# Graph network on one Trainium2 core: SyncE fetches four pairs of tiles per layer row by row, by row numbers in registers

## The chip, the core and the metric

The kernel runs on one core of one Trainium2 chip. The metric is the device time of one execution in microseconds (us). Five engines run their own instruction streams and meet at semaphores: TensorE (PE in the profile), VectorE (DVE), ScalarE (ACT), GpSimd (POOL) and SyncE (SP), which in this kernel only issues DMAs.

## The reference

Three layers of a relational graph network over 6250 nodes of 256 numbers and 100000 edges, sorted by target node, then a layer norm.

```python
ew = edge_attr @ edge_w + edge_b
inv_cnt = [1.0 / max(segment_sum(edge_type == i, dst), 1.0) for i in range(3)]
for l in range(3):
    residual = x
    msg = relu(x[src] * ew)
    out = zeros((n, 256))
    for i in range(3):
        h = segment_sum(msg * (edge_type == i)[:, None], dst) * inv_cnt[i][:, None]
        out = out + h @ weights[l, i]
    out = out + x @ roots[l] + biases[l]
    x = residual + relu(out)
return layernorm(x0 + x)
```

## The kernel before

The edges are cut into 782 tiles of 128, handled as 391 pairs per layer. One step of a layer handles one pair (`q` in the code; `l` is the layer).

- **GpSimd gathers.** For each tile one indirect DMA (`gather`, L620 to L626) fetches the 128 rows `x[src]`, 1 KB each, by the row numbers in a column of `idx`, into one of twelve places of the ring `xg` (`XR = 12`, so six pairs). Before it refills a place it waits on `s_sc` until TensorE has summed the pair that lay there. GpSimd does nothing else once the kernel has started up.
- **TensorE** computes the edge weights of a pair (L771), with the transposed edge attributes from `at`; **VectorE** waits for both gathers and multiplies the rows in place by these weights (L1092, called the product below); **ScalarE** applies relu (L694); TensorE sums the rows per target node and relation with a 0/1 matrix `S` (L790, `collect`); VectorE adds these sums to the accumulator `acc` (L948), whose column it takes from a number that it has loaded into a register (L1082).
- **Blocks.** 49 blocks of 128 target nodes own 384 columns each in both halves of `acc`. When the last tile that touches a block is in (`starts[k]`), TensorE multiplies the block's sums by the weights (L842), VectorE finishes the nodes, SyncE stores them to `x` of the next layer, and ScalarE clears the block's columns (L721). The block that finishes first (`k = 0` in the order of finishing, at step 14) is the short one at the end of `acc`, columns from `384 * (NB - 1)`.
- **SyncE** runs in step with TensorE, since most of its DMAs wait for a semaphore of TensorE. Per two steps it issues, in layer 0, one load of edge attributes (L523) and one store of their transposed form (L529), and in layers 1 and 2 one load of that form (L535). Per block it issues one load of the block's x (L541) and one store of the result (L555), in layer 2 also a second load (L547). Its DMAs are issued in program order: one that waits, or takes long to issue, holds up all behind it.
- **Between layers** GpSimd waits until all stores of the new x have landed, and only then gathers again.

The order of the tiles is written by `plan()`. Steps are in the same place in every engine's program, and nothing but semaphores sets the pace.

Of the kernel before, what the change touches and what calls it, by code (L numbers as in the profile page):

```python
# [62 lines left out]
def gnn_program(nc, x_in, src, dst, edge_attr, edge_type, weights, roots, biases, edge_w, edge_b,  # L63
# [5 lines left out]
    DVE = mybir.EngineType.DVE  # L69
# [15 lines left out]
    PAD = 1000000  # L85
    BR = 196
# [25 lines left out]
    with ctx:  # L112
# [104 lines left out]
        s_st, s_sq, s_no = sem("s_st"), sem("s_sq"), sem("s_no")  # L217
        s_dm, s_d2, s_hz = sem("s_dm"), sem("s_d2"), sem("s_hz")
# [15 lines left out]
        def tile(n):  # L234

            return head_tile(order[n // 4]) + n % 4

# [263 lines left out]
        def _(eng):  # L501
# [55 lines left out]
            for g in range(3):  # L557
                load_attr(g)

            def fast():  # L560
                for l in range(L):
                    late = (13, 9, 15)[l]
                    for q in range(-4, end):
                        if l == 0 and q % 2 == 0:
                            if 3 <= q // 2 + 4 < NG:
                                load_attr(q // 2 + 4)
                            if 0 <= q // 2 < NG:
                                keep_attr(q // 2)
                        if l and q % 2 == 0 and q // 2 + 2 < NG:
                            reload_attr(l, q // 2 + 2)  # L570
                        if q == 0:
                            for i in range(TB if l else 0):
                                eng.wait_ge(s_xo[i], 16 * uses(l, i, TB, NB))
                            if l == 0:
                                load_weights(l)
                            for k in range(XB):
                                load_x(l, k)
                            if l == L - 1:
                                load_x0(0)
                                load_x0(1)  # L580
                        if q == 8 and l:
                            load_weights(l)
                        for k in starting(q, 8 if l else 12):
                            if k + XB < NB:
                                load_x(l, k + XB)
                        for k in starting(q, 9):
                            if l == L - 1 and k + 2 < NB:
                                load_x0(k + 2)
                        for k in starting(q, late):
                            store(l, k)  # L590
# [10 lines left out]
        def _(eng):  # L601
# [18 lines left out]
            def gather(l, j):  # L620
                n = l * NT + j
                if n >= XR:
                    eng.wait_ge(s_sc, 2 * ((n - XR) // 2 + 1))
                eng.indirect_dma_start(  # L624
                    out=xg[:, n % XR, :], out_offset=None, in_=xs[l],
                    in_offset=bass.IndirectOffsetOnAxis(ap=idx[:, tile(j):tile(j) + 1], axis=0)).then_inc(s_g[n % XR], 16)  # L626

            eng.wait_ge(s_src, 16)
            for j in range(XR):
                gather(0, j)  # L630

            def fast():
                for l in range(L):
# [3 lines left out]
                    for j in range(0 if l else XR, NT):  # L637
                        gather(l, j)
# [5 lines left out]
        def _(eng):  # L644
# [42 lines left out]
            def fast():  # L687
                for l in range(L):
                    for q in range(-6, end):
                        Q = l * NP + q  # L690
                        if 0 <= q < NP:
                            eng.wait_ge(s_m, Q + 1)
                            v = xg[:, (2 * Q) % XR:(2 * Q) % XR + 2, :]
# [23 lines left out]
                        if l < L - 1:  # L717
                            for k in starting(q, 5 if l else 7):
                                eng.wait_ge(s_d1, NB * l + k + 1)
                                a, b = columns(blocks[k])  # L720
# [12 lines left out]
        def _(eng):  # L733
# [41 lines left out]
            def collect(l, q):  # L775
# [11 lines left out]
                for i in range(2):  # L787
                    n = 2 * V + i
                    for h in range(2):
                        last = eng.matmul(pA[V % 2][:, 192 * i + 96 * h:192 * i + 96 * h + 96],  # L790
                                          xg[:, n % XR, 128 * h:128 * h + 128], S[:, slot(l, 2 * q + i), :],
# [81 lines left out]
        def _(eng):  # L873
# [200 lines left out]
            def fast():  # L1074
                for l in range(L):
                    todo = {}
                    for q in range(-6, end):
# [8 lines left out]
                        if 0 <= q < NP:  # L1086
                            for i in range(2):
                                n = 2 * Q + i
                                eng.wait_ge(s_g[n % XR], 16 * (n // XR + 1))
                            eng.wait_ge(s_e, Q + 1)  # L1090
                            v = xg[:, (2 * Q) % XR:(2 * Q) % XR + 2, :]
# [83 lines left out]
```

## Time and profile before

| | before |
|---|---|
| median of 3 runs (lowest to highest) | 2993.76 us (2991.76 to 2998.16) |
| the profiled execution's own time | 2995.98 us |
| its span, first to last instruction | 2994.3 us |
| granted TensorE clock, mean | 0.956 |
| busy share of the span: PE, PEld, DVE, ACT, POOL | 87%, 80%, 71%, 43%, 74% |
| gathers (DMA_INDIRECT on POOL) | 2346, of 0.95 us each |
| DMA issues on SP | 1147 |

The own time lies 1.68 us above the span, and 2.2 us above the median of the runs. Shares of busy time count only what the engines themselves compute: the time in which a sequencer loads a register, waits for a semaphore or issues a DMA is not in them, and SP has no busy time at all for that reason.

### The profile page before, as it was taken

To read this page: it belongs to the slowest core of one execution; us is meant where nothing else is said; L and a number is where in the kernel's file an instruction comes from. 1 tells how busy PE (TensorE), PEld (TensorE's weight loads), DVE (VectorE), ACT (ScalarE), POOL (GpSimd) and SP (SyncE) were. 2 spreads that over 40 slices of the span, in tenths; PEclk is the share of its full clock that TensorE was granted. 3 is DMA by queue.
4 is the path that set the end of the run, shared out by engine and by line. 5 is a ranking of instruction groups with operands and counts; after the bars stand their busy time and mean duration, and the time that the engine had idled before them with its cause. 6 is when DMAs were issued, how large, how long until landed. Compare 5 with 4: busy or idle time off the path is not lost. (4 is left out here: it accounts for less than half of the span.)

```text
span 2994.3 us, 59606 instructions
## 1 busy us (share of the span) xinstructions
PE 2611.1 (87%) x18388; PEld 2409.2 (80%) x18388; DVE 2127.0 (71%) x5989; ACT 1279.4 (43%) x2735; POOL 2227.1 (74%) x2363
## 2 busy tenths in 40 slices
PE   7899999999999788888898888878888888888887
PEld 6888888988889677778787788867778888877786
DVE  6777777777777566666666666656767777777776
ACT  6667777767666323233333333323223233233332
POOL 6777777777777677777777777767777777777775
PEclk9999999999999899999999999989999999999999
DMA  6555655555565445445554555444555555555553
GB/s 170 156 159 156 160 159 158 161 158 160 160 161 159 142 142 146 143 146 146 146 147 146 147 146 146 144 136 145 149 148 152 154 149 156 150 156 150 157 152 111
DMA packets 317059, 451.39 MB, mean 151 GB/s; under 512 B 156127, under 2 KB 203718, under 8 KB 316742
## 3 DMA queue, kind: packets, MB, share of 16 engines
q0 software_dynamic: 112608, 307.65, 36.5%
q1 hardware_dynamic: 203604, 139.69, 16.3%
q8 instruction: 156, 2.56, 0.3%
q14 instruction: 161, 1.32, 0.1%
q10 hardware_dynamic: 530, 0.18, 0.0%
HBM read 402.46 MB, written 44.82 MB: 149 GB/s over the span
## 5 line engine op out<-in xcount | busy, mean ns | idle before, releaser
L624 POOL DMA_INDIRECT xg<-x,idx x1564 | 1481.9, 948 | 503.5 <-issue 340.1
L694 ACT ACTIVATE xg<-xg 128x512 f32<-128x512 f32 x1173 | 739.3, 630 | 1668.3 <-DVE xg L1092 1654.4
L790 PE MATMUL bank<-S,xg 128*128 128x96 f32 x9384 | 1331.0, 287 | 131.0 <-DVE acc L948 97.3
L1092 DVE TENSOR_TENSOR xg<-xg,bank 128x512 f32<-128x512 f32 x1173 | 805.2, 686 | 791.6 <-issue 344.4
L790 PEld LDWEIGHTS bank<-S,xg 128*128 128x128 f32 x9384 | 1195.8, 199 | 201.7 <-ACT xg L694 173.1
L771 PE MATMUL bank<-wsb,at 128*128 128x256 f32 x4692 | 917.9, 319 | 175.4 <-DVE xg L1092 143.5
L624 POOL DMA_INDIRECT xg<-in_x_dram,idx x782 | 742.9, 950 | 243.7 <-issue 163.9
L771 PEld LDWEIGHTS bank<-wsb,at 128*128 128x128 f32 x4692 | 690.0, 198 | 255.6 <-issue 108.6
L948 DVE TENSOR_TENSOR acc<-acc,bank 128x192 f32 x2346 | 813.9, 347 | 30.2 <-DVE acc L948 13.8
L842 PE MATMUL bank<-W,acc 128*128 128x256 f32 (+1 forms) x1764 | 496.0, 405 | 3.0 <-DVE acc L948 3.0
L842 PEld LDWEIGHTS bank<-W,acc 128*128 128x128 f32 (+1 forms) x1764 | 380.4, 255 | 5.4 <-DVE acc L948 3.5
L929 DVE TENSOR_TENSOR S<-bank,kr 128x384 f32<-128x384 f32 x588 | 323.0, 549 | 0.0
L713 ACT ACTIVATE oh_a<-iota,lo 128x128 bf16<-128x128 bf16 x782 | 266.1, 388 | 0.0
L965 DVE SCALAR_TENSOR_TENSOR t<-bank,inv,t 128x256 f32<-128x256 f32 (+1 forms) x441 | 209.1, 474 | 15.8 <-PE bank L842 15.5
L842 PE MATMUL bank<-W,xT 128*128 128x256 f32 (+1 forms) x588 | 170.2, 416 | 0.0
L747 PE MATMUL bank<-ident,hs 128*64 128x128 f32 x782 | 121.7, 280 | 19.0 <-ACT xT L702 15.8
L842 PEld LDWEIGHTS bank<-W,xT 128*128 128x128 f32 (+1 forms) x588 | 111.9, 209 | 10.7
L668 ACT ACTIVATE at<-bank 64x512 fp32r<-64x512 f32 x196 | 112.3, 573 | 4.6 <-PE bank L747 4.5
L747 PEld LDWEIGHTS bank<-ident,hs 128*64 128x64 f32 x782 | 86.4, 120 | 24.8 <-DVE hs L885 18.8
L785 PE MATMUL bank<-oh_b,oh_a 128*128 128x12 bf16 x782 | 80.1, 174 | 12.3 <-issue 8.2
L721 ACT ACTIVATE acc<-zcol 128x768 f32<-128x768 f32 (+1 forms) x98 | 81.4, 831 | 14.2 <-PE bank L842 14.2
L815 PE MATMUL bank<-ident,xblk 128*128 128x128 f32 (+1 forms) x294 | 59.0, 284 | 23.3 <-ACT at L668 23.2
(64 smaller groups left out, 687.2 us busy)
## 6 DMA issues: line engine op xcount, KB each, us to landing
at<-attr_t SPq DMA_DIRECT2D x390, 128.0 KB
xg<-x,idx POOLq DMA_INDIRECT x1564
attr_t<-at SPq DMA_DIRECT2D x195, 128.0 KB
xg<-in_x_dram,idx POOLq DMA_INDIRECT x782
hs<-in_edge_attr_dram SPq DMA_DIRECT2D x194, 64.0 KB
x<-t SPq DMA_DIRECT2D x96, 128.0 KB
xblk<-x SPq DMA_DIRECT2D x96, 128.0 KB
xblk<-in_x_dram SPq DMA_DIRECT2D x48, 128.0 KB
```

Source lines behind the costliest of these rows:

```text
L624: eng.indirect_dma_start(out=xg[:, n % XR, :], out_offset=None, in_=xs[l], in_offset=bass.IndirectOffsetOnAxis(ap=idx[:, tile(j):tile(j) + ...
L668: eng.activation(at[0:64, g % TR, 0:w], pT[0:64, 0:w], ACT.Copy).then_inc(s_atc, 1)
L694: eng.activation(v, v, ACT.Relu).then_inc(s_r, 1)
L713: eng.activation(oh_a[:, j % AR, :], iota[:, 1:129], ACT.Sign, bias=lo[:, tile(j):tile(j) + 1]).then_inc(s_oh, 1)
L747: last = eng.transpose(pT[0:64, 128 * i:128 * i + 128], hs[:, g % 3, i, :], ident[:, :])
L771: last = eng.matmul(pE[Q % 2][:, 256 * i:256 * i + 256], at[:, sl, c:c + 128], wsb[:, p, :], start=(p == 0), stop=(p == 1))
L790: last = eng.matmul(pA[V % 2][:, 192 * i + 96 * h:192 * i + 96 * h + 96], xg[:, n % XR, 128 * h:128 * h + 128], S[:, slot(l, 2 * q + i), : ...
L842: last = eng.matmul(o, a, W[:, 2 * (r % 4) + h, :], start=(h == 0), stop=(h == 1))
L929: eng.tensor_tensor(S[:, at4:at4 + w, :], steps_of[:, 1:WK + 1].unsqueeze(1).to_broadcast([128, w, WK]), kr[:, c:c + w].unsqueeze(2).to_br ...
L948: eng.tensor_tensor(a, a, pA[V % 2][:, 192 * i:192 * i + 192] .rearrange("p (h w) -> p h w", h=2), ALU.add).then_inc(s_acc, 1)
L965: return eng.scalar_tensor_tensor(tt, products(k, m), inv[0:n, 3 * blocks[k] + r:3 * blocks[k] + r + 1], tt, ALU.mult, ALU.add)
L1092: eng.tensor_tensor(v, v, pE[Q % 2][:, :].rearrange("p (i d) -> p i d", i=2), ALU.mult).then_inc(s_m, 1)
```

## The change

Per layer, four of the 391 pairs (113, 204, 295 and 386, `BY_ROW`) are no longer gathered by GpSimd. SyncE fetches their 256 rows by one DMA of one row (1 KB) each. It first loads the pair's row numbers from DRAM into SBUF (`load_list`, two DMAs of 512 bytes), then reads four of these numbers into registers at a time, computes a byte offset from each, and issues a DMA with that offset (`load_rows`). The 64 groups of four rows of a pair are spread over 84 of SyncE's steps: for pair 113 over steps 26 to 109, for a later one from 4 steps behind the pair before it to 4 steps ahead of its own.

The rows go into columns of `acc` that belong to the short block, which is finished at step 14: 256 columns in both halves hold the pair, the 128 behind them the row numbers. So ScalarE clears this block at the layer's last step and no longer right behind its products. GpSimd leaves the four pairs out and numbers its ring places by the pairs that are left; VectorE waits for such a pair on `s_row`, and product, relu and sums work on `acc` in place of `xg`.

```diff
+    BY_ROW = (113, 204, 295, 386)
...
+        def pool_pair(l, q):
+            return l * (NP - len(BY_ROW)) + q - sum(p < q for p in BY_ROW)
+        pairs = [(l, q) for l in range(L) for q in range(NP) if q not in BY_ROW]
+        row_buf = acc[:, :, 384 * (NB - 1):384 * (NB - 1) + D]
+        def rows_of(l, q):
+            if q in BY_ROW:
+                return row_buf
+            a = 2 * pool_pair(l, q) % XR
+            return xg[:, a:a + 2, :]
+        def row_list(i, h):
+            a = 384 * (NB - 1) + D
+            return acc[32 * h:32 * h + 1, i % 2, a:a + 128].bitcast(I32)
...
+            def load_list(l, i):
+                for h in range(2):
+                    a = 128 * tile(2 * BY_ROW[i] + h)
+                    eng.dma_start(row_list(i, h), src[a:a + 128].rearrange("(q p) -> q p", q=1)).then_inc(s_sr[i % 2], 16)
+            def load_rows(l, i, c):
+                if c == 0:
+                    eng.wait_ge(s_sr[i % 2], 32 * (l * len(BY_ROW[i % 2::2]) + i // 2 + 1))
+                if c == 0 and i:
+                    eng.wait_ge(s_sc, l * NT + 2 * (BY_ROW[i - 1] + 1))
+                if c == 32 and i + 1 < len(BY_ROW):
+                    load_list(l, i + 1)
+                h, e = c // 32, 4 * (c % 32)
+                _, vals = nc.values_load_multi_w_load_instructions(
+                    row_list(i, h)[:, e:e + 4], engines=[SP], min_val=0, max_val=N - 1,
+                    skip_runtime_bounds_check_because="a node's number")
+                for r, v in enumerate(vals):
+                    eng.dma_start(row_buf[e + r:e + r + 1, h, :], xs[l][bass.ds(v, 1), :]).then_inc(s_row[l], 16)
+            def row_turn(q):
+                for i, p in enumerate(BY_ROW):
+                    b = BY_ROW[i - 1] + 4 if i else p - 87
+                    if b <= q < b + 84 and (q == b or (q - b) * 64 // 84 > (q - b - 1) * 64 // 84):
+                        return i, (q - b) * 64 // 84
+                return None
...
+                        if q == BY_ROW[0] - 89:
+                            eng.wait_ge(s_d1, NB * l + 1)
+                            load_list(l, 0)
+                        if row_turn(q):
+                            load_rows(l, *row_turn(q))
...
-            def gather(l, j):
-                n = l * NT + j
-                if n >= XR:
-                    eng.wait_ge(s_sc, 2 * ((n - XR) // 2 + 1))
+            def gather(l, q, i):
+                P = pool_pair(l, q)
+                n = 2 * P + i
+                if P >= XR // 2 and i == 0:
+                    before, pair = pairs[P - XR // 2]
+                    eng.wait_ge(s_sc, before * NT + 2 * (pair + 1))
...
-                            for k in starting(q, 5 if l else 7):
+                            for k in ([0] if q == NP - 1 else []) + [k for k in starting(q, 5 if l else 7) if k]:
                                 eng.wait_ge(s_d1, NB * l + k + 1)
+                                if k == 0:
+                                    eng.wait_ge(s_sc, l * NT + 2 * (BY_ROW[-1] + 1))
...
-                            for i in range(2):
-                                n = 2 * Q + i
+                            if q in BY_ROW:
+                                eng.wait_ge(s_row[l], 16 * 256 * (BY_ROW.index(q) + 1))
+                            for i in range(0 if q in BY_ROW else 2):
+                                n = 2 * pool_pair(l, q) + i
                                 eng.wait_ge(s_g[n % XR], 16 * (n // XR + 1))
```

SyncE in layer 0, steps 24 to 28, before (`hs` holds raw edge attributes, `attr_t` their transposed form in DRAM, `xblk` a block's x, `t` a block's result):

```order
L529 DMA attr_t<-at 64x512 [waits s_atc]
L523 DMA hs<-in_edge_attr_dram 128x4x32 [waits s_tr]
L529 DMA attr_t<-at 64x512 [waits s_atc]
L541 DMA xblk<-in_x_dram 128x256 [waits s_rd]
L555 DMA x<-t 106x256 [waits s_rd]
L523 DMA hs<-in_edge_attr_dram 128x4x32 [waits s_tr]
```

The same place in the changed program, behind the two DMAs for the row numbers (its lines L544, L550 and L562 are L523, L529 and L541 of before):

```order
L544 DMA hs<-in_edge_attr_dram 128x4x32 [waits s_tr]
L550 DMA attr_t<-at 64x512 [waits s_atc]
L593 TENSOR_LOAD acc [waits s_sr0]
L597 ISA
L597 DMA acc<-in_x_dram 1x256
L597 ISA
L597 DMA acc<-in_x_dram 1x256
L597 ISA
L597 DMA acc<-in_x_dram 1x256
L597 ISA
L597 DMA acc<-in_x_dram 1x256
L562 DMA xblk<-in_x_dram 128x256 [waits s_rd]
```

Between the attribute DMAs of two steps there now stand one or two such groups of nine instructions: one register load, then four times a calculation (ISA) and a DMA of one row. The block's load and store stand behind a group too.

GpSimd, start and gathers of all layers, before:

```order
L624 DMA xg<-in_x_dram,idx 128x256 x12
L493 TENSOR_LOAD flag
L493 ISA x2
L494 COMPARE_AND_BRANCH
L624 DMA xg<-in_x_dram,idx 128x256 x770
L624 DMA xg<-x,idx 128x256 x1564
```

and changed:

```order
L679 DMA xg<-in_x_dram,idx 128x256 x12
L514 TENSOR_LOAD flag
L514 ISA x2
L515 COMPARE_AND_BRANCH
L679 DMA xg<-in_x_dram,idx 128x256 x762
L679 DMA xg<-x,idx 128x256 x1548
```

Eight gathers per layer are gone; nothing takes their place on GpSimd.

VectorE at pair 386 of layer 0, before:

```order
L1082 TENSOR_LOAD brow
L1092 TENSOR_TENSOR xg<-xg,bank 128x512 [waits s_e,s_g5,s_g4]
L948 ISA [waits s_acc,s_sc]
L948 TENSOR_TENSOR acc<-acc,bank 128x2x96
L929 TENSOR_TENSOR S<-bank,kr 128x384 [waits s_sc]
```

and changed:

```order
L1141 TENSOR_LOAD brow
L1153 TENSOR_TENSOR acc<-acc,bank 128x2x256 [waits s_e,s_row0]
L1007 ISA [waits s_acc,s_sc]
L1007 TENSOR_TENSOR acc<-acc,bank 128x2x96
L988 TENSOR_TENSOR S<-bank,kr 128x384 [waits s_sc]
```

The product of such a pair stands where it stood and has its size; it waits for SyncE's rows in place of two gathers.

## Rows read from the trace of the kernel before

**Rows 1.** Timeline of POOL: start us, us, what [idle before <- releaser].

```profile
1003.17 0.95 POOL L624 DMA_INDIRECT xg<-x,idx  x1 [12.90 <-DMA x<-t]
...
1500.67 0.95 POOL L624 DMA_INDIRECT xg<-x,idx  x1 [0.30 <-PE bank L790]
1501.92 0.95 POOL L624 DMA_INDIRECT xg<-x,idx  x1 [0.30 <-issue]
1503.17 0.95 POOL L624 DMA_INDIRECT xg<-x,idx  x1 [0.30 <-issue]
...
1979.39 0.94 POOL L624 DMA_INDIRECT xg<-x,idx  x1 [0.30 <-issue]
```

**Rows 2.** Waits of POOL, 1010 to 1980 us: us in total, times, longest us.

```profile
POOL xg L624 <- issue: 169.1, 555, 0.3
POOL xg L624 <- PE bank L790: 67.6, 222, 0.3
```

**Rows 3.** Busy time by stretch: layer 0, layer 1.

```profile
20.00:990.00 970.00, 898.29 (x7161) 846.78 (x7160) 745.62 (x2465) 675.48 (x1692) 730.50 (x771) 0.98 0.59 159
1003.00:1980.00 977.00, 842.54 (x5543) 765.51 (x5544) 655.11 (x1599) 294.20 (x486) 738.91 (x782) 0.95 0.50 146
```

**Rows 4.** Waits of DVE, 1010 to 1980 us.

```profile
DVE xg L1092 <- DMA xg<-x,idx: 127.2, 150, 9.3
```

**Rows 5.** Timeline of PE, sums of one pair each, 1499 to 1506 us.

```profile
1499.29 1.03 PE L790 MATMUL bank<-S,xg 128*128 128x96 f32 x8
...
1501.58 1.03 PE L790 MATMUL bank<-S,xg 128*128 128x96 f32 x8
```

**Rows 6.** Timeline of all engines: products at the end of layer 0.

```profile
984.41 0.69 DVE L1092 TENSOR_TENSOR xg<-xg,bank 128x512 f32<-128x512 f32 x1 [3.18 <-DMA xg<-in_x_dram,idx]
...
986.20 0.68 DVE L1092 TENSOR_TENSOR xg<-xg,bank 128x512 f32<-128x512 f32 x1
...
988.07 0.69 DVE L1092 TENSOR_TENSOR xg<-xg,bank 128x512 f32<-128x512 f32 x1 [0.37 <-issue]
...
990.66 0.69 DVE L1092 TENSOR_TENSOR xg<-xg,bank 128x512 f32<-128x512 f32 x1
```

**Rows 7.** DMA issues on SP by line: duration ns min/median/max, first and last start us.

```profile
L523 SPq DMA_DIRECT2D hs<-in_edge_attr_dram x196: 368/377/1035, 2.7 to 971.5; - x196
L529 SPq DMA_DIRECT2D attr_t<-at x196: 445/516/1703, 20.2 to 990.1; - x196
L535 SPq DMA_DIRECT2D at<-attr_t x392: 444/450/1367, 1001.7 to 2961.6; - x196
L541 SPq DMA_DIRECT2D xblk<-x x98: 310/334/435, 1003.7 to 2911.2; - x98
L541 SPq DMA_DIRECT2D xblk<-in_x_dram x49: 336/584/1352, 24.1 to 939.2; - x49
L555 SPq DMA_DIRECT2D x<-t x98: 298/438/1611, 80.9 to 1992.6; - x98
```

**Rows 8.** A one-row DMA on ACT's queue; register loads and calculations of sequencers.

```profile
L651 ACTq DMA_DIRECT2D acc<-in_L_gnn_edge_b_dram x1: 597/597/597, 3.2 to 3.2; - x1
...
L493 SPq TENSOR_LOAD <-flag x1: 468/468/468, 14.5 to 14.5; - x1
...
L493 SPq FUSED_REGOPS  x1: 188/188/188, 15.0 to 15.0; - x1
...
L1082 DVEq TENSOR_LOAD <-brow x588: 339/560/1225, 18.4 to 2976.3; - x196
...
L948 DVEq FUSED_REGOPS  x2346: 46/46/46, 24.1 to 2981.5; - x196
```

**Rows 9.** Timeline of SP in layer 0, two DMAs behind each other.

```profile
771.00 0.38 SPq L523 DMA_DIRECT2D hs<-in_edge_attr_dram  x1
771.42 0.52 SPq L529 DMA_DIRECT2D attr_t<-at  x1
```

**Rows 10.** Waits of SP, whole span.

```profile
SPq L535 <- PE bank L771: 1070.8, 274, 9.1
SPq L523 <- PE bank L747: 698.6, 191, 8.7
```

More of the change, by code:

```diff
@@ L68, in gnn_program @@
     AX = mybir.AxisListType
-    DVE = mybir.EngineType.DVE
+    DVE, SP = mybir.EngineType.DVE, mybir.EngineType.SP
     N, E, D, R, L = 6250, 100000, 256, 3, 3
@@ L217, in gnn_program @@
         s_st, s_sq, s_no = sem("s_st"), sem("s_sq"), sem("s_no")
+        s_sr = sems("s_sr", 2)
+        s_row = sems("s_row", L)
         s_dm, s_d2, s_hz = sem("s_dm"), sem("s_d2"), sem("s_hz")
@@ L618, in _ @@
                                   base=b, pattern=[[-1, 128]], channel_multiplier=1).then_inc(s_df, 1)
-            def gather(l, j):
-                n = l * NT + j
-                if n >= XR:
-                    eng.wait_ge(s_sc, 2 * ((n - XR) // 2 + 1))
+            def gather(l, q, i):
[4 more added lines that the diff above has]
+                    eng.wait_ge(s_sc, before * NT + 2 * (pair + 1))
+                c = tile(2 * q + i)
                 eng.indirect_dma_start(
                     out=xg[:, n % XR, :], out_offset=None, in_=xs[l],
-                    in_offset=bass.IndirectOffsetOnAxis(ap=idx[:, tile(j):tile(j) + 1], axis=0)).then_inc(s_g[n % XR], 16)
+                    in_offset=bass.IndirectOffsetOnAxis(ap=idx[:, c:c + 1], axis=0)).then_inc(s_g[n % XR], 16)
             eng.wait_ge(s_src, 16)
-            for j in range(XR):
-                gather(0, j)
+            for l, q in pairs[0:XR // 2]:
+                gather(l, q, 0)
+                gather(l, q, 1)
             def fast():
@@ L636, in fast @@
                             eng.wait_ge(s_xo[i], 16 * uses(l, i, TB, NB))
-                    for j in range(0 if l else XR, NT):
-                        gather(l, j)
+                    for q in range(0 if l else XR // 2, NP):
+                        if q not in BY_ROW:
+                            gather(l, q, 0)
+                            gather(l, q, 1)
             both(eng, "gpsimd", fast)
@@ L692, in fast @@
                             eng.wait_ge(s_m, Q + 1)
-                            v = xg[:, (2 * Q) % XR:(2 * Q) % XR + 2, :]
+                            v = rows_of(l, q)
                             eng.activation(v, v, ACT.Relu).then_inc(s_r, 1)
@@ L787, in collect @@
                 for i in range(2):
-                    n = 2 * V + i
                     for h in range(2):
                         last = eng.matmul(pA[V % 2][:, 192 * i + 96 * h:192 * i + 96 * h + 96],
-                                          xg[:, n % XR, 128 * h:128 * h + 128], S[:, slot(l, 2 * q + i), :],
+                                          rows_of(l, q)[:, i, 128 * h:128 * h + 128], S[:, slot(l, 2 * q + i), :],
                                           start=True, stop=True)
@@ L1086, in fast @@
                         if 0 <= q < NP:
[L1087 to L1088 removed]
+                            if q in BY_ROW:
+                                eng.wait_ge(s_row[l], 16 * 256 * (BY_ROW.index(q) + 1))
+                            for i in range(0 if q in BY_ROW else 2):
+                                n = 2 * pool_pair(l, q) + i
                                 eng.wait_ge(s_g[n % XR], 16 * (n // XR + 1))
                             eng.wait_ge(s_e, Q + 1)
[L1091 removed]
+                            v = rows_of(l, q)
                             eng.tensor_tensor(v, v, pE[Q % 2][:, :].rearrange("p (i d) -> p i d", i=2),
```

## The prediction

> **What bounds the kernel now.** The busy shares point at PE (87%), and for this change they mislead. I read the timeline of GpSimd first, then its waits, then the same for the engines that use the rows.
>
> GpSimd's gathers start 1.25 us apart, 0.95 us in the gather and 0.30 us until the next one [rows 1]. Over layer 1, the first starts at 1003.17 us and the last of 782 at 1979.39 us: 976.22 / 781 = 1.250 us each, so not one came late. The waits say the same: none of the 777 idle stretches of that layer was longer than 0.3 us, whether it is put down to PE or to nothing [rows 2]. The busy share of 74% is only 0.95 / 1.25 with the layer ends taken off. The three layers hold 2346 such periods, 2932 us of the 2994.3.
>
> No other engine is at its limit. In layer 1 PE computes 843 of 977 us, VectorE 655, in layer 0 PE 898 of 970 [rows 3]. VectorE waited 127 us in layer 1 for rows still under way [rows 4]. And the places of the ring are free early. Counted from the layer's first gather, the one at 1500.67 us is tile (1500.67 - 1003.17) / 1.25 = 398, the first of pair 199, and may go once pair 193 is summed. The sums on PE at 1499.29 us are pair 195's, those at 1501.58 us pair 196's [rows 5]. So pair 194 was done too; by the pace of 2.3 to 2.5 us per pair, pair 193 had been done for 4 to 6 us.
>
> **What the change removes.** Eight gathers per layer, 24 in all, from the queue that sets the pace: 24 x 1.25 = **30.0 us**. A step of TensorE and VectorE must then take 2.5 x 387 / 391 = 2.47 us on average in place of 2.50.
>
> **Can the others take one pair more between two gathers?** At a row-by-row pair they have an extra pair's work while rows keep coming at 2.5 us per pair. How fast they go with rows at hand shows behind a late gather: after an idle time of 3.18 us the products start 1.79, 1.87 and 2.59 us apart, 2.08 us on average [rows 6]. So with one pair extra, the product of the pair behind it starts 2 x 2.08 - 2.50 = 1.7 us late, and each later pair makes up 0.4 us. That is less than the 4 us by which the ring's places are free early, so GpSimd isn't stopped: no cost there. Only at a layer's end is it seen, because pair 386 is followed by just four pairs: 1.7 - 3 x 0.42 = 0.4 us late at pair 390, **1.2 us** for three layers.
>
> **What the change adds to SyncE** is the term on which all rests, and the trace has no DMA by a register's value.
>
> - Register load of four numbers: VectorE's takes 0.56 us, SyncE's only one (of one number) 0.47 us; the gap behind an instruction is 0.04 us (771.00 + 0.38 to 771.42). I take 0.51 with its gap [rows 8, 9].
> - Calculation: 0.046 us on VectorE; with its gap 0.08. SyncE's own, longer one took 0.19 right behind a load, so at most 0.15 more per group [rows 8].
> - One-row DMA: SyncE's loads of a block's x, the same 1 KB rows into SBUF, take 0.334 us for 128 rows when nothing was issued just ahead, 0.31 at the least (the block of 106 rows) [rows 7]. The only DMA of one row is ScalarE's, 0.597 us, one of six issued back to back beside SyncE's own at the start [rows 8]. These are the bounds, 0.31 and 0.60. I take 0.33, the row with the same kind of transfer, with the queue in the state in which a register load just ahead leaves it; with its gap 0.37.
>
> One row is then 0.08 + 0.37 = 0.45 us, a group 0.51 + 4 x 0.45 = 2.31 us, a pair 64 x 2.31 = 148 us.
>
> SyncE's own work in 84 steps, medians plus gaps: in layer 0 42 x (0.377 + 0.516 + 0.08) + 10.5 blocks x (0.584 + 0.438 + 0.08) = 41 + 12 = 53 us; in layer 1 42 x 0.49 + 10.5 x 0.85 = 29 us; in layer 2, with a second load of 0.37 per block, 33 us [rows 7]. The 84 steps last 84 x 2.47 = 208 us. Layer 0: 148 + 53 = 201. Layers 1 and 2: 177 and 181. It fits, by 7 us in layer 0 and some 29 in the others, and before this work SyncE mostly waited: 1070.8 and 698.6 us on its two main waits [rows 10]. So all of the new work lies in time in which SyncE waited.
>
> The cover is thin, so its limits matter. Behind a group stand the attribute loads for TensorE and, in layer 0, for ScalarE. A group is 2.3 us, so such a load goes out up to 2.3 us later (4.6 where two groups stand together); layer 1 has it for step q + 3 at step q, some 7 us ahead. With a one-row DMA of x us, layer 0 falls behind within the 84 steps from (208 - 53) / 64 = 2.42 us per group, which is x = 0.36, and over the whole 91 steps (225 us, own work 57) from 2.62 us, x = 0.41. Layer 1 bears x = 0.51, layer 2 0.49.
>
> The rest costs nothing. The product on `acc` has the size of that on `xg` (0.69 us [rows 6]). ScalarE's clear of the short block moves to the last step, behind the last relu, where ScalarE waits for the last block anyway; the next layer asks for it only with all other clears. The load of a list is two short DMAs per pair, in front of work that is 32 groups away. The 3072 rows, 3 MB, were moved before too.
>
> **Sum.** 2994.3 - 30.0 + 1.2 = 2965.5 us of span, 2967.2 of own time (1.68 above). The profiled run was 2.2 us above the median, so the median to expect is **2965.0**.
>
> The Trainium skill ("DMA: Bandwidth & Descriptors", the table on the faster descriptor path, in the section "Why a DMA increments its semaphore by 16 and not by 1") speaks against my price: it gives 512 sequencer cycles for a DMA copy on the generations before that path. With the 1.2 GHz of "Advanced Engine Details and Errata", section "Clock Domains", that is an estimate of 0.43 us. This trace half agrees: the attribute loads take 0.45 us, the loads of x 0.33. By it a group would be 2.7 us and the kernel some 20 us above my sum.
>
> **Rivals.**
>
> 1. *SyncE is late in layer 0 alone* (x between 0.41 and 0.46). For it: the attribute loads at 0.450 us, the stores at 0.438 and 0.516 behind another DMA [rows 7]. Over a cycle of 91 steps SyncE's excess sets the pace. At x = 0.43 a group is 0.51 + 4 x 0.55 = 2.71 us, the cycle 57 + 173 = 230 against 225: 4 x 5 = 20 us, time 2985. At x = 0.435 the 30 us are used up (2994); at 0.46 it is 3009. Against it: there the DMA waits behind a large one; here nothing large stands ahead. Chance 0.15, of which two thirds below 2988. The skill's 0.43 us, above, would be this case.
> 2. *SyncE becomes the bound everywhere* (the other side). One mechanism: a one-row DMA costs SyncE 0.60 us, as ScalarE's did [rows 8]. A group is 0.51 + 4 x 0.72 = 3.39 us, a pair 217. Cycles of 57 + 217 = 274, 32 + 217 = 249 and 36 + 217 = 253 us stand against 225: 4 x (49 + 24 + 28) = 404 us, time 3370. It is slower than before from x = 0.435 on, by layer 0 alone, and from x = 0.51 on the other layers are over their limit too. Attribute loads would be late, and TensorE wait for them. For it: the only row of its form. Against it: its neighbours on that queue took 0.45 with 32 rows, so 0.15 of it may be the queue's state; and a register's value may add time that no row shows. Chance 0.16.
> 3. *The extra pair does stop GpSimd*, or rows come late by a few us and the product waits: each of the 12 pairs gives back 1 to 2.5 us. Time 2977 to 2994. Against it: the ring's 4 us and more. Chance 0.06.
> 4. *No effect*: GpSimd's period stretches, since it gathers less but the DMA engines or its own issue slow down. Nothing for it; the period was 1.25 in all layers. Chance 0.03.
>
> The forecast itself, 2961 to 2974, has 0.60.
>
> **How the numbers follow.** A measurement of this kernel tells about 0.2% (6 us) from no change. Faster: 0.60, two thirds of rival 1, most of rival 3: 0.75. Same: the rest of rival 3, rival 4 and a piece of rival 1: 0.07. Slower: 0.18. The range has to take in most of rival 1 and rival 3: 2961 to 3005 holds 0.81.
>
> **What would show it.** Right: 2322 gathers, still 1.25 us apart in every layer; gathering of each layer 10 us shorter; a group of nine instructions on SyncE near 2.3 us, its one-row DMA near 0.33 us; SyncE still waiting for PE on its attribute DMAs within the 84 steps; VectorE with no wait to speak of at the four products; layer ends within a us of before. Wrong: gaps on POOL above 0.3 us that end with PE, and PE waiting for attribute loads, above all in layer 0, where the margin is 7 us in 208; or a wait of VectorE for the rows.

## The result

| | before | changed |
|---|---|---|
| median (lowest to highest) | 2992.78 us (2991.76 to 2998.16), 4 runs | 3093.73 us (3087.56 to 3098.62), 4 runs |
| the profiled execution's own time | 2995.98 us | 3096.11 us |
| its span | 2994.3 us | 3094.3 us |
| granted TensorE clock, mean | 0.956 | 0.936 |
| gathers on POOL | 2346 | 2322 |

The changed kernel is slower: ratio 1.0332, 95% interval 1.0309 to 1.0356. The forecast was 2965.0 us, the range ended at 3005. The experiments ran on four chips. On those of e6 to e9 and of e10 to e12 the kernel before takes 2994.2 and 2994.8 us, so their times can be set beside each other. On those of e1 to e4 and of e5 the same kernel takes 3602 and 3605 us; of these runs only ratios, differences between themselves and the lengths of single instructions are used.

**Where the 100 us lie.** The starts of the gathers again give the layers, from the first to the last. Layer 0 takes 1081.1 us instead of 984.8 (+96.3), the pause behind it 23.6 instead of 13.9 (+9.8), layer 1 967.3 instead of 976.2 (-8.9), the next pause 14.5 instead of 15.7 (-1.2), layer 2 983.0 instead of 979.7 (+3.3), the tail 20.2 instead of 19.5 (+0.7). The sum is +100.0, the difference of the two spans. So layer 1 shows the gain that was forecast for every layer, and layer 0 a loss ten times as large.

Waits of the changed kernel in layer 0, 5 to 1086 us (us in total, times, longest us):

```profile
ACT hs L718 <- DMA hs<-in_edge_attr_dram: 264.7, 124, 6.1
DVE hs L944 <- ACT hs L718: 185.7, 103, 5.3
POOL xg L679 <- PE bank L849: 159.1, 158, 5.8
```

Before, GpSimd had no wait of more than 0.3 us in layer 1 [rows 2] and few in layer 0. Here it waits up to 5.8 us for a place in its ring, that is for the sums on PE. The first row shows what is late ahead of PE: ScalarE waits 124 times for edge attributes that SyncE loads from DRAM.

The waits of SP over the whole span, to be read beside [rows 10] (L544 is L523 of before, L556 is L535):

```profile
SPq L556 <- PE bank L831: 159.5, 83, 9.6
SPq L544 <- PE bank L807: 67.8, 26, 8.3
```

SyncE's idle time on its two main waits, 1769 us before, is 227 us now. Within the second window of row loads, 316 to 581 us, what is left of it is this:

```profile
SPq L550 <- ACT at L726: 2.4, 5, 0.8
SPq L544 <- PE bank L807: 0.5, 2, 0.3
```

With 2.9 us of waiting in 265 us SyncE is the bound there. In the chain that ended last SP's queue (SPq) has as large a share as PE; in that of the kernel before it does not occur:

```profile
SPq 28%; PE 28%; DMA 14%; issue 13%; POOL 12%; DVE 3%; ACT 2%; DVEq 0%
```

**One stall, followed.** Timelines of SP, ACT, PE and POOL in layer 0 of the changed kernel (start us, us, what; loads of registers have no row of their own in this view and show as gaps):

```profile
426.64 0.37 SPq L562 DMA_DIRECT2D xblk<-in_x_dram  x1
428.28 1.50 SPq L597 DMA_DIRECT2D acc<-in_x_dram  x4
429.83 0.38 SPq L576 DMA_DIRECT2D x<-t  x1
430.26 0.43 SPq L544 DMA_DIRECT2D hs<-in_edge_attr_dram  x1
430.73 0.68 SPq L550 DMA_DIRECT2D attr_t<-at  x1
433.27 1.54 SPq L597 DMA_DIRECT2D acc<-in_x_dram  x4
434.86 0.41 SPq L544 DMA_DIRECT2D hs<-in_edge_attr_dram  x1
```

```profile
433.35 0.31 ACT L718 ACTIVATE hs<-hs 128x128 fp32r<-128x128 f32 x1 [4.91 <-DMA hs<-in_edge_attr_dram]
```

```profile
435.15 0.20 PE L845 MATMUL bank<-oh_b,oh_a 128*128 128x12 bf16 x2 [3.84 <-ACT oh_a L771]
```

```profile
432.92 0.94 POOL L679 DMA_INDIRECT xg<-in_x_dram,idx  x1 [0.30 <-issue]
437.48 0.94 POOL L679 DMA_INDIRECT xg<-in_x_dram,idx  x1 [3.62 <-PE bank L849]
```

The view shows no wait of SP here: each gap is a register load and the first address behind it, 1.27 us from 427.01 to 428.28 and 1.86 us from 431.41 to 433.27, and four rows take 1.50 us and more. The attribute load behind them goes out at 430.26. ScalarE, idle for 4.91 us, gets its attributes at 433.35. Its next work stands behind them in program order, and PE, idle for 3.84 us, waits for that work until 435.15. Only then come the sums that free a place of the ring, and GpSimd stands for 3.62 us from 433.86 on. An attribute load serves two pairs, 5.0 us of GpSimd's time; in this window SyncE has 42 of them in 265 us, one every 6.3 us.

**The price of the load.** Durations of SP's register loads by stretch (min/median/max in ns): layer 0, window of the first pair and of the second; layer 1, the same two.

```profile
L593 SPq TENSOR_LOAD <-acc x64: 465/827/1241, 80.4 to 300.9; - x64
...
L593 SPq TENSOR_LOAD <-acc x64: 1062/1666/1815, 315.9 to 577.3; - x64
...
L593 SPq TENSOR_LOAD <-acc x64: 485/738/753, 1176.0 to 1381.6; - x64
...
L593 SPq TENSOR_LOAD <-acc x64: 1032/1307/1328, 1401.7 to 1620.9; - x64
```

The loads of SyncE have 0.47 us, without the gap, in the prediction. None of the four medians is near it, and the second pair's loads are about 0.6 us longer than the first pair's in layer 1 and 0.8 in layer 0. The rest of a row is cheap, in the first pair's window (L597, three instructions for each of 256 rows):

```profile
L597 SPq FUSED_REGOPS  x256: 37/37/48, 81.3 to 302.7; - x128
L597 SPq MOVE acc<-in_x_dram x256: 29/29/38, 81.4 to 302.8; - x128
L597 SPq DMA_DIRECT2D acc<-in_x_dram x256: 224/228/297, 81.5 to 302.9; - x128
```

From the first load to the last row, a group of four takes 2.54 us (mean of 64) in the windows of pairs 1 and 3 of layer 0 and 3.20 in those of pairs 2 and 4; the means of the loads in them are 0.82 and 1.49 us. In layer 1 the groups take 2.36 and 2.93 us. These windows show when GpSimd stood. What its gathers start later than 1.25 us behind the one before, called its gaps below, adds up to 2, 45, 12 and 41 us in the four windows of layer 0, at most 0.5 us in each of those of layer 1, and 1, 8, 2 and 5 us in layer 2.

### The profile page after: what moved, and what is told of

Its sections match the earlier page's. It is cut to its first block, busy times and chain, and to the rows that moved or that the text cites. A ratio compares the mean times of both kernels' runs of the same rounds, so it can differ in the third digit from the quotient of the medians.

```text
span 3094.3 us, 69601 instructions
## 1 busy us (share of the span) xinstructions
PE 2634.8 (85%) x18388; PEld 2450.5 (79%) x18388; DVE 2140.4 (69%) x5989; ACT 1280.9 (41%) x2735; POOL 2205.3 (71%) x2339
## 4 chain that ended last, share of the span: by engine, by line
SPq 28%; PE 28%; DMA 14%; issue 13%; POOL 12%; DVE 3%; ACT 2%; DVEq 0%
PE bank L849 14%; POOL xg L679 12%; SPq L597 11%; SPq L593 11%; DMA xg<-x,idx 9%; PE bank L901 6%; PE bank L831 6%; DMA hs<-in_edge_attr_dram 2%; SPq L550 2%; DMA at<-attr_t 2%; SPq L544 1%; DVE acc L1007 1%; SPq L556 1%; PE bank L807 1%; DVE xg L1153 1%
## 5 line engine op out<-in xcount | busy, mean ns | idle before, releaser
L752 ACT ACTIVATE xg<-xg 128x512 f32<-128x512 f32 x1161 | 729.1, 628 | 1464.9 <-DVE xg L1153 1460.6
L849 PEld LDWEIGHTS bank<-S,xg 128*128 128x128 f32 x9288 | 1209.9, 203 | 154.0 <-ACT xg L752 132.1
L1153 DVE TENSOR_TENSOR xg<-xg,bank 128x512 f32<-128x512 f32 x1161 | 795.2, 685 | 582.4 <-DMA xg<-x,idx 301.3
L831 PE MATMUL bank<-wsb,at 128*128 128x256 f32 x4692 | 936.3, 324 | 210.1 <-DVE xg L1153 104.0
L831 PEld LDWEIGHTS bank<-wsb,at 128*128 128x128 f32 x4692 | 705.9, 202 | 284.4 <-DMA at<-attr_t 113.4
L901 PE MATMUL bank<-W,acc 128*128 128x256 f32 (+1 forms) x1764 | 503.8, 410 | 3.1 <-DVE acc L1007 3.1
L944 DVE TENSOR_TENSOR hs<-hs 128x128 f32<-128x128 f32 x196 | 57.0, 291 | 190.8 <-ACT hs L718 189.8
L718 ACT ACTIVATE hs<-hs 128x128 fp32r<-128x128 f32 x196 | 59.8, 306 | 270.4 <-DMA hs<-in_edge_attr_dram 269.3
L845 PEld LDWEIGHTS bank<-oh_b,oh_a 128*128 128x128 bf16 x782 | 51.7, 106 | 90.4 <-ACT xg L752 74.0
```

The source lines that it names most:

```text
L752: eng.activation(v, v, ACT.Relu).then_inc(s_r, 1)
L831: last = eng.matmul(pE[Q % 2][:, 256 * i:256 * i + 256], at[:, sl, c:c + 128], wsb[:, p, :], start=(p == 0), stop=(p == 1))
L901: last = eng.matmul(o, a, W[:, 2 * (r % 4) + h, :], start=(h == 0), stop=(h == 1))
L1153: eng.tensor_tensor(v, v, pE[Q % 2][:, :].rearrange("p (i d) -> p i d", i=2), ALU.mult).then_inc(s_m, 1)
```

## The experiments

Pairs 113, 204, 295 and 386 are called pairs 1 to 4. Pairs 1 and 3 have their row numbers in the first half of `acc`, pairs 2 and 4 in the second.

**e1, e2: without the loads.** e1 leaves out the register loads, the row DMAs and the wait for them; e2 issues the row DMAs with row numbers fixed when the program is built, without loads or calculations.

```diff
-                for r, v in enumerate(vals):
+                for r, v in enumerate(range(97 * c, 97 * c + 4)):       # e2
-                    eng.dma_start(row_buf[e + r:e + r + 1, h, :], xs[l][bass.ds(v, 1), :]).then_inc(s_row[l], 16)
+                    pass                                                # e1
```

> Leaves out the row loads of the four pairs and their register loads: SyncE does none of the new work, VectorE does not wait for rows, GpSimd gathers as in the change. Theory A (GpSimd's gain is real and SyncE's lateness alone eats it): 2322 gathers 1.25 us apart in all layers, time 2963 to 2967. Rival (the shorter gather list gains nothing, because another engine or the extra pair stops GpSimd): 2980 or more, with gaps on POOL that end with PE.

> Fetches rows with fixed numbers, so it leaves out the register loads and calculations; the same 3072 one-row DMAs are issued. Theory A (the register load, 0.9 to 1.15 us on average against 0.51 in the prediction's sum, is what makes SyncE late): without it a group is some 1.1 to 1.3 us, layer 0 has 208 - 53 - 80 = 75 us to spare, time as without rows, 2963 to 2970. Rival (the 3072 small DMAs themselves, through contention with attribute loads and gathers, cost the time): above 3000.

Measured: e1 3576.55 us, ratio 0.9927 (0.9911 to 0.9944); e2 3620.69 us, ratio 1.0058 (1.0041 to 1.0075). Leaving out 24 gathers is worth 26 us on this chip, so most of the 30 us is a real gain. The gathers were not 1.25 us apart throughout, as expected; GpSimd waited 515 us for the sums on PE and 262 us for what the profile calls remote. With the 3072 row DMAs the time is 44 us longer than in e1. That is the side of the rival: on this chip these DMAs cost time without any register load. e9 and e11 below show no such cost on the chips on which the kernel before takes 2994 us.

**e3, e5: where the list starts.** The second half of `acc` lies 18846 columns of 4 bytes, 75384 bytes, behind the first, which is 8 past a multiple of 16. The first list starts at byte 74752 of `acc` in its partition, a multiple of 16; so the second starts 8 bytes past one. (That `acc` itself starts at a multiple of 16 isn't on record; e12, with all four starts, bears it out.) e3 moves the second list by two columns, so that both start at a multiple; e5 moves the first one instead, so that neither does.

```diff
-            a = 384 * (NB - 1) + D
+            a = 384 * (NB - 1) + D + 2 * (i % 2)          # e3
+            a = 384 * (NB - 1) + D + 2 * ((i + 1) % 2)    # e5
```

> One edit: the second list of row numbers lies two columns further on, so that it starts at a multiple of 16 bytes as the first does. In the profile of the change loads from the first list take 0.49 to 0.74 us and from the second 1.06 to 1.31 us (layer 1). Theory A (a load of four numbers that crosses a 16-byte boundary is read twice): loads of the second and fourth pair fall by 0.57 us, layer 0 loses its 45 to 50 us of gaps at each of these two pairs down to the 6 to 12 us of the others, time 2995 to 3025. Rival (loads of the second list are slow for another reason, as the steps they fall in or the semaphore before them): loads stay above 1 us and the time at 3090.

> One edit: the first list is moved two columns on too, so that both lists start 8 bytes behind a multiple of 16 (all else as in the change). Theory A (a load of four numbers that crosses a 16-byte boundary is read twice, 0.57 us more): in layer 1 loads of the first and third pair rise from 0.49 to 0.74 to 1.06 to 1.31 us, like those of the second and fourth; layer 0 loses some 45 us at each of its pairs, and on a chip like the one of the change's profile the time goes from 3094 to 3150 to 3180 us. Rival (the second list's loads are slow for another reason): loads of the first and third pair stay, time as the change, 3094.

Measured: e3 3749.78 us, ratio 1.0398 (1.0381 to 1.0415); e5 3944.43 us, ratio 1.0945 (1.09 to 1.0989). All 768 loads of each, e3 first:

```profile
L595 SPq TENSOR_LOAD <-acc x768: 3/707/1510, 97.7 to 3723.8; - x192
```

```profile
L595 SPq TENSOR_LOAD <-acc x768: 3/1239/2694, 97.5 to 3919.9; - x192
```

The start of the list decides the length of the load, and the half of `acc` that it is in does not: with all lists off the median is 1.24 us, with none 0.71, and the times are 195 us apart. The loads of 3 ns and the like, 92 of e3's below 0.1 us, stand only in the profiles of these chips and stay unexplained. The changed kernel itself wasn't run on them, so what e3 gives back there is not known; its 4.0% above the kernel before misses the 2995 to 3025 us that were expected. e10 is the same kernel on a chip of the faster kind.

**e4: rows in layers 1 and 2 only,** with the lists as in the change. The pairs and windows stand in a table by layer, whose first row is empty here.

```diff
-    BY_ROW = (113, 204, 295, 386)
+    ROWS = [[], [(113, 26, 84), (204, 117, 84), (295, 208, 84), (386, 299, 84)], [(113, 26, 84), (204, 117, 84), (295, 208, 84), (386, 299, 84)]]
```

> Layer 0 gathers all its pairs as before; rows go by SyncE in layers 1 and 2 alone, the second list unaligned as in the change. Theory A (layer 0 is where the time goes; layers 1 and 2 gain): layer 0 as before, layer 1 some 10 us shorter, layer 2 some 2 us longer as in the profile of the change to 7 shorter, time 2975 to 2990. Rival (the loss has a part that is in all layers and only shows in layer 0): above 3000.

Measured: 3712.28 us, ratio 1.0319 (1.0284 to 1.0354). Layer 0 took 1199.1 us, 9 more than in e1, with its eight gathers more, and layers 1 and 2 took 54 and 61 us more than in e1. With aligned lists (e3) they took 35 and 39 us more, with fixed rows (e2) 15 and 12. So on that chip rows cost in every layer, which is the rival's side, while in the main comparison layer 1 gained. For the main comparison this run decides nothing; e7 has its aligned form on the chip of e6.

**e6: the change again**, on the chip of e7 to e9.

> The changed kernel itself (its four row windows written as a table), as the reference point for the runs beside it. Both theories: a register load of 0.5 to 0.75 us from the first list and 0.57 us more from the second; the time 3 to 6 per cent above the kernel before. If it stands at the ratio 1.033 of the main comparison, the costs on this chip can be read in the same terms; if it is well above that, only differences between the runs of this call count.

Measured: 3094.44 us, ratio 1.0352 (1.0325 to 1.0378), the main result once more; layers of 1077.1, 967.9 and 981.9 us.

**e10: both lists aligned, nothing else** (the edit of e3).

> The changed kernel with the second list two columns further, so that both lists start at a multiple of 16 bytes; four numbers to a load, rows in all three layers. Theory (the loss is SyncE's in layer 0 and scales with the length of its loads): the loads of pairs 2 and 4 fall from 1.07 to 1.8 us to those of pairs 1 and 3, layer 0 loses only what pairs 1 and 3 lost in the changed kernel, twice over: 2 x (6 + 12) = some 35 us instead of 110, layer 2 its 15 us; the time 3094 - 75 - 12, about 3005 us, ratio 1.00 to 1.01. Rival (SyncE's time is short in layer 0 whatever the list, the loss moves to the other pairs): layer 0 still 60 us and more too long, ratio 1.015 to 1.03.

Measured: 3000.3 us, ratio 1.0016 (1.0006 to 1.0026). Loads of pairs 1 and 2 in layer 0:

```profile
L595 SPq TENSOR_LOAD <-acc x64: 465/760/1201, 80.5 to 301.1; - x64
...
L595 SPq TENSOR_LOAD <-acc x64: 487/748/1171, 316.2 to 537.6; - x64
```

The groups now take 2.53 to 2.54 us in layer 0, and its gaps fall from 111 us (e6) to 34; the kernel before has 8. Two columns are worth 94 us, almost the whole loss. (e6 and e10 ran on two chips, on which the kernel before differs by 0.6 us.) The rival, that the loss only moves to the other pairs, falls. GpSimd's and ScalarE's waits in layer 0 (5 to 980 us) are still there, smaller:

```profile
ACT hs L719 <- DMA hs<-in_edge_attr_dram: 185.2, 105, 4.5
POOL xg L680 <- PE bank L850: 68.0, 128, 5.3
```

**e8: the load ahead of its step's transfers,** lists as in the change. **e11: the same with both lists aligned.**

```diff
                     for q in range(-4, end):
+                        if row_turn(l, q):
+                            load_numbers(l, *row_turn(l, q))
                         if l == 0 and q % 2 == 0:
                             if 3 <= q // 2 + 4 < NG:
                                 load_attr(q // 2 + 4)
```

`load_numbers` holds the wait for the list and the register load, taken out of `load_rows`, which keeps the addresses and the DMAs.

> The changed kernel with each register load moved to the head of its step, ahead of the attribute transfers, the lists as in the changed kernel. Theory A' (a load is longer right behind a transfer of many descriptors, because it waits for that transfer's issue to drain): the loads of the steps with attribute transfers fall from 0.74 to about 0.5 us (first list) and from 1.31 to about 1.07 (second), and the time falls by some 10 to 30 us against the changed kernel. Rival: it is longer behind any other work of the queue, and the load stays as long (the wait only moves); time within 0.3 per cent of the changed kernel.

> Both: aligned lists and each load ahead of its step's attribute transfers. If both savings are SyncE's and add up, the loads fall to 0.49 to 0.56 us in most steps, the group of four rows to 2.3 us and less in layers 1 and 2, layer 0's gaps shrink to 10 us or less, and the time comes to 2965 to 2985 us, the forecast of the prediction. If the gap in layer 0 has another cause than SyncE's own time, it stays above 3000 us.

Measured: e8 3039.42 us, ratio 1.0158 (1.0141 to 1.0175), 55 us below the change (e6, the same chip), more than expected. All loads together fell from 781 to 683 us. e11: 2967.3 us, ratio 0.9907 (0.989 to 0.9923), as expected; its loads sum to 446 us, with e10's at 550 (the same chip). Layer 0 takes 977.6 us in e11, with gaps of 10 us, nearly those of the kernel before. Waits in layer 0 of e11 (5 to 980 us):

```profile
POOL xg L687 <- PE bank L857: 34.2, 97, 3.5
ACT hs L726 <- DMA hs<-in_edge_attr_dram: 5.5, 3, 2.7
```

ScalarE's wait for attributes is back at its size of before (6.5 us, twice). Moving the loads out from behind the attribute transfers thus removed the rest of layer 0's loss.

**e9: eight numbers to a load,** aligned, so 32 loads per pair; the order in the step as in the change.

```diff
-                _, vals = nc.values_load_multi_w_load_instructions(
-                    row_list(i, h)[:, e:e + 4], engines=[SP], min_val=0, max_val=N - 1,
+                if e % PER == 0:                                        # PER = 8
+                    _, held[0] = nc.values_load_multi_w_load_instructions(
+                        row_list(i, h)[:, e:e + PER], engines=[SP], min_val=0, max_val=N - 1,
...
-                for r, v in enumerate(vals):
+                for r, v in enumerate(held[0][e % PER:e % PER + 4]):
```

> Aligned lists and eight numbers to one register load, 32 loads per pair of tiles instead of 64. If the price is per instruction, a load stays at 0.5 to 0.75 us and SyncE gets half of the 148 x 0.5 us per pair back, and the time falls 0.5 to 1.5 per cent below the aligned version of four numbers. If the price is per 16 bytes read, a load takes 1.05 to 1.3 us and the time is that of the aligned version.

Measured: 2964.44 us, ratio 0.9902 (0.9886 to 0.9919). Loads of the first pair of layer 1, and GpSimd's waits in layer 0 (5 to 980 us):

```profile
L598 SPq TENSOR_LOAD <-acc x32: 711/958/979, 1059.5 to 1263.0; - x32
```

```profile
POOL xg L683 <- PE bank L853: 33.4, 96, 2.8
```

Four more aligned numbers cost 0.22 us (0.96 against 0.74), between the two prices that were expected, and nearer to a price per instruction. With half as many loads, all of SyncE's loads sum to 369 us, against e10's 550. All three layers are short: 975.2, 967.1 and 968.8 us.

**e7: rows in layers 1 and 2, aligned** (the edits of e4 and e3).

> Rows only in layers 1 and 2, both lists starting at a multiple of 16 bytes, layer 0 fetched by GpSimd alone. Theory A (the loss sits on SyncE, in the length of the register loads: 2.2 us of its time per group of four rows with aligned lists, which layers 1 and 2 can give): well below the changed kernel, and at or below the kernel before, ratio 0.993 to 1.01. Rival B (the rows or their wait on VectorE cost in themselves, wherever they stand): layers 1 and 2 keep about the length that they have in the changed kernel, and only layer 0 gets its loss back.

Measured: 2973.25 us, ratio 0.993 (0.9914 to 0.9947). 21 us less than before for 16 gathers, 16 x 1.25 = 20. Rows that SyncE has the time for cost nothing elsewhere on this chip: rival B falls.

**e12: the load by itself,** rows in layers 1 and 2.

```diff
-            a = 384 * (NB - 1) + D
+            a = 384 * (NB - 1) + D + (0, 3, 2, 1)[i]
-    PER = 8
+    PER = (8, 4, 8)
```

> Measures the load alone: rows in layers 1 and 2 only, the lists of pairs 1 to 4 at 0, 4, 8 and 12 bytes past a multiple of 16, with four numbers to a load in layer 1 and eight in layer 2. If a load pays for each 16 bytes that it touches, four numbers cost 0.56 us behind a row at offset 0 and 1.13 at each of 4, 8 and 12, and eight numbers 0.79 at 0 and one step more at the others. If it pays for numbers that are fetched one by one once the start is off, the price grows from four to eight numbers by about 0.5 us or more at 4, 8 and 12, and by 0.23 at 0.

Measured (one run, 2986.26 us): the loads of pairs 1, 2, 3 and 4, starting 0, 4, 8 and 12 bytes past a multiple of 16, with four numbers (layer 1) and then with eight (layer 2):

```profile
L598 SPq TENSOR_LOAD <-acc x64: 466/742/756, 1067.4 to 1274.9; - x64
...
L598 SPq TENSOR_LOAD <-acc x64: 1042/1308/1341, 1294.8 to 1516.1; - x64
...
L598 SPq TENSOR_LOAD <-acc x64: 1039/1308/1349, 1527.7 to 1747.8; - x64
...
L598 SPq TENSOR_LOAD <-acc x64: 1035/1306/1331, 1758.8 to 1977.1; - x64
...
L598 SPq TENSOR_LOAD <-acc x32: 711/958/982, 2062.7 to 2270.1; - x32
...
L598 SPq TENSOR_LOAD <-acc x32: 1835/2106/2191, 2292.2 to 2500.0; - x32
...
L598 SPq TENSOR_LOAD <-acc x32: 1857/2104/2137, 2516.6 to 2727.2; - x32
...
L598 SPq TENSOR_LOAD <-acc x32: 1859/2106/2127, 2742.9 to 2950.4; - x32
```

It makes no difference whether the start is off by 4, 8 or 12 bytes, and the price grows by 0.80 us for four more numbers, 0.20 each, against 0.22 for all four where the start is aligned. Pair 3 has its list in the first half of `acc` and is as slow as pairs 2 and 4, so once more it isn't the half. The numbers fit a load that takes them one by one off a multiple of 16, and four at a time on one. The one-number load of [rows 8] agrees with both: 0.47 + 3 x 0.20 = 1.07 us for four singly, and 0.47 us against the 0.49 of four at once. Only four and eight numbers were tried, and aligned loads of eight all started at multiples of 32 bytes. A price per 16 bytes touched would have grown by one step of 0.57 at most and falls.

This run also shows what unaligned lists cost in layer 1 when three pairs in a row have them: the layer takes 980.6 us, against 968.4 with aligned lists (e7), with gaps of 2, 8 and 3 us in the three windows.

## Why the prediction was wrong

**The step that failed** is the first item of what the change adds to SyncE: "Register load of four numbers: [...] I take 0.51 with its gap." It measured 0.70 and 1.28 us with its gap in layer 1, and 0.87 and 1.53 in layer 0, for aligned and unaligned lists. There are two reasons, and each has an experiment of its own.

1. *The unaligned list*: +0.57 us for each of four numbers' loads, half of all loads (e12, e10). The prediction took its price from two rows [rows 8] of which SP's loads one number only, and VectorE's four-number load, at 0.56 us, isn't SyncE's. It never asked where the list starts in memory.
2. *The place behind a transfer*: the same aligned load takes 0.49 us behind a load of x, 0.56 behind rows, 0.74 behind the attribute load of layers 1 and 2, and 1.03 behind the store of layer 0 (medians of e10). The prediction reckoned with "the state in which a register load just ahead leaves" the queue for the DMAs, and not with the state in which the attribute DMA leaves it for the load. Moving the load was worth 55 us with half of the lists unaligned (e8) and 33 us with all aligned (e11). Why the load is longer there is not shown. It isn't the size: the load of x and the store of a result move 128 KB like the attribute transfers, and behind either the aligned load takes 0.49 us (e10, e11).

**A bound was put on the wrong term.** All doubt was priced through x, the one-row DMA, from 0.31 to 0.60 us. It took 0.228, cheaper than either end, and a whole row 0.42 us instead of 0.45. The Trainium skill ("DMA: Bandwidth & Descriptors", section "Why a DMA increments its semaphore by 16 and not by 1") has 512 cycles for a DMA copy on the generations before its faster path, 0.43 us by the estimate in the prediction; the trace does not agree. The load was given a single value, with no other end. The Trainium skill ("DMA: Bandwidth & Descriptors", section "Latency and other measured facts") has about 600 ns as the floor of a register load; the trace shows less, 0.46 us for the shortest and 0.49 to 0.56 as medians away from the attribute transfers. The Trainium skill ("Runtime: NRT & Kernel Launch", section "Instruction fetch mechanics") puts a register load at about 200 ns per register even in bulk, and speaks of loads from HBM, while these lists lie in SBUF. In size the runs agree for unaligned lists (0.20 for each further number), and not for aligned ones (0.22 for four).

**The mechanism was that of rival 1**, SyncE late in layer 0 and nearly in it alone: attributes late, then ScalarE, VectorE and PE, then GpSimd's ring. But rival 1 made SyncE late by a dear one-row DMA, and it was the load. One sum of the rival is off too: at x = 0.46 a group is 2.83 us and the cycle 57 + 181 = 238 us, so the time would be 2965 + 4 x 13 = 3017 us and not 3009, outside the range that was given. The limits on the length of a group hold, with one correction. The prediction had two: 2.42 us per group to keep up within the 84 steps, 2.62 over the whole cycle of 91, and let the second set the pace. The measured groups decide for the first. At 3.20 us a window ends (3.20 - 2.42) x 64 = 50 us late, and GpSimd's gaps in it were 45 and 41; at 2.54 it is 8 us, and the gaps were 2 and 12 in the change, 1, 5, 9 and 4 in e10. By the second limit they would be 37 and none. The measured gaps lie within 9 us of the first limit's. The loads that e8 and e11 moved fit it as well: they took 0.20 to 0.25 us off the mean load of a window of layer 0, which leaves (3.20 - 0.24 - 2.42) x 64 = 35 us for unaligned lists, where the gaps were 29 and 27, and nothing for aligned ones, where they were about 1 us or less. Layer 2 has its first limit at (208 - 33) / 64 = 2.73 and lost 5 and 8 us in windows with groups of 2.94; layer 1, at 2.80 against 2.93, lost none with every second pair unaligned, and 13 us in e12 with three in a row. With aligned lists, at 2.54, the time was near no change (e10); what made 100 us of it was the unaligned list.

**What was right.** GpSimd's period stayed at 1.25 us, and 24 gathers are worth their 30 us once SyncE keeps up: e9 came to 2964.4 us where the forecast was 2965.0. That this agrees to 0.6 us is luck in part, as e9's runs lie between 2962.1 and 2966.5, and the term for the layer ends, 1.2 us, is too small to be seen in them. SyncE's own work of 53 us nearly fits: in the window of pair 2, 53 + 64 x 3.20 = 258 us, and it lasted 265, of which it waited 3. The extra pair stopped nobody (rival 3): layer 1 had five gaps, of 1.1 us in all. The pause behind layer 0, 23.6 us, is not in any term (the prediction had the layer ends within a us of before); it stays at 23 in e10, where the last window also runs past the last gather (1007 against 1005 us), and falls to 13 and 14 us in e9 and e11, where it ends earlier. So it goes with SyncE's lateness too. VectorE waited 8.9 us for rows in layers 1 and 2 and 5.4 us in layer 0.

Left open: why the kernel before takes 3602 and 3605 us on two of the chips. GpSimd waits there for something that the profile calls remote (262 us in e1), and on the chip of the main comparison it doesn't. Open as well is why rows cost time in every layer on those chips, even where no register is loaded (e2).

## What to carry to other kernels

Before a queue is given work through registers, write down where its list starts and what stands ahead of each load. In these runs four 4-byte numbers, loaded behind rows, took SyncE 0.56 us from a multiple of 16 bytes and 1.13 us from 4, 8 or 12 bytes past one. Loading eight numbers at a time, or moving the loads ahead of the attribute transfers, each brought the aligned kernel from 3000 us to 2964 and 2967; both together were not tried. And where a forecast rests on a margin of 7 us in 208, every term of that sum needs two ends, not just the one that looks strangest.

A queue that mostly waits can be full after a small change: 1769 us of waiting over 2994 did not say what one layer can bear. The limit must be worked out for the layer with most work of its own and for the stretch in which the new work lies, not over the pause behind it.

## What was unexpected of the hardware

- SyncE's register load of four numbers: 0.49 to 0.56 us aligned, 1.06 to 1.13 unaligned by 4, 8 or 12 bytes; of eight: 0.71 to 0.80 and 1.86 to 1.95 (medians behind a load of x and behind rows, e12).
- The aligned load of four right behind an attribute transfer: 0.18 us more than behind rows in layers 1 and 2, 0.47 in layer 0 (e10). Behind other DMAs of the same 128 KB it is not longer.
- A DMA of one 1 KB row with its address in a register occupies the queue for 0.228 us, the one with a fixed address 0.252 (e2; on its chip the one with a register takes 0.228 too, e3), and neither shows the 0.597 us of [rows 8] again.
- With GpSimd's gaps TensorE's clock fell too. Its granted clock was 0.98 in layer 0 before [rows 3]; in the changed kernel, by stretch (span, then PE, PEld, DVE, ACT, POOL busy, clock, DMA share, GB/s), first the windows of pairs 1 and 2 and then the layer:

```profile
80.00:303.00 223.00, 203.08 (x1589) 192.02 (x1590) 166.81 (x549) 151.91 (x378) 168.07 (x178) 0.95 0.58 156
316.00:581.00 265.00, 224.13 (x1633) 211.09 (x1632) 171.92 (x560) 153.30 (x384) 167.39 (x177) 0.89 0.49 132
```

```profile
20.00:1086.00 1066.00, 938.59 (x7128) 885.92 (x7127) 748.32 (x2447) 668.32 (x1674) 722.56 (x763) 0.93 0.54 144
```

PE was busy 939 us in layer 0 against 898 before, for nearly the same matmuls, and less densely; a mean of 0.89 lies between the two levels of 2.4 and 1.2 GHz, so the throttle granted the lower one for part of the stretch. e10 has 0.98 and 898 us again, in the 985 us from 20 to 1005. So the lower clock comes with the gaps; whether it also lengthens them was not tried apart.
